# Set-up of a fused residual-stack kernel: W1's loads on ScalarE's queue, E1 products by block, part of the table chain on GpSimd, all weight quarters completed on VectorE

## What is computed

```python
x = x + L0(x, lengths)          # long convolution: K = 2 Re sum_n Cs exp(dtA * l), by head; masked by length
x = x @ W1.T + 2 * gated low-rank term (8 experts, rank 16, top 2 of the logits)
x = x @ W2.T + 0.5 * low-rank term (5 labels, rank 32)
x = x @ (quantised(W3 + delta) + delta).T      # delta = 0.5 * B3 @ A3 (rank 64), thresholds from a 64-entry codebook
```

## Time and profile before

| quantity | value |
|---|---|
| median of 3 runs | 1047.79 us (1047.1 to 1048.24) |
| profiled execution, its own time | 1049.61 us |
| its span | 1047.8 us |
| TensorE busy | 1004.1 us (96%), 4855 instructions |
| VectorE busy | 850.6 us (81%) |
| ScalarE busy | 428.5 us (41%) |
| GpSimd busy | 292.0 us (28%) |
| W1's loads | 8 of 512 KB, median 7.4 us from issue to landing |
| W2's loads | 8 of 512 KB |
| B3 and A3 loads | 2 of 256 KB each |

### The profile page before, as it was taken

One profiled execution on the slowest core, in us unless ns is written; L12 is line 12 of the kernel. 1 busy time (PEld: TensorE's weight loads), 2 busy tenths in 40 slices (PEclk: granted clock), 3 DMA queues, 4 the chain that ended last, 5 costly groups with the idle time before them and its releaser, 6 DMA issues.

```text
span 1047.8 us, 16630 instructions
## 1 busy us (share of the span) xinstructions
PE 1004.1 (96%) x4855; PEld 800.8 (76%) x4855; DVE 850.6 (81%) x1678; ACT 428.5 (41%) x847; POOL 292.0 (28%) x319
## 2 busy tenths in 40 slices
PE   2999999999899999999999999999999999999997
PEld 1555556978688878888888888888888888888885
DVE  5888888979896488878888888888888888888862
ACT  3212222222257454454445444544354535553531
POOL 2200304373435323222332233222322232223100
PEclk9999999999999999999999999999999999999999
DMA  8601000010201335454544455445544454445311
GB/s 257 164 21 61 20 6 35 1 41 1 40 1 21 64 59 104 80 89 75 104 84 84 77 103 87 79 81 97 94 76 84 88 100 74 88 81 103 59 39 41
DMA packets 316659, 74.97 MB, mean 72 GB/s; under 512 B 292490, under 2 KB 309194, under 8 KB 316626
## 3 DMA queue, kind: packets, MB, share of 16 engines
q1 hardware_dynamic: 316626, 74.56, 36.2%
HBM read 57.61 MB, written 16.91 MB: 71 GB/s over the span
## 4 chain that ended last, share of the span: by engine, by line
PE 75%; DVE 10%; issue 9%; ACT 2%; DMA 2%; DVEq 1%; SPq 0%; ACTq 0%
PE bank L647 33%; PE bank L637 10%; PE bank L774 6%; PE bank L823 5%; PE bank L668 4%; PE bank L617 4%; PE bank L606 4%; PE bank L628 3%; DVE quant L1464 3%; PE bank L674 2%; DVE step_t L1459 1%; DVE quant L1505 1%; DVE vq L1478 1%; PE bank L658 1%; DVE quant L1504 1%
## 5 line engine op out<-in xcount | busy, mean ns | idle before, releaser
L647 PE MATMUL bank<-Mh,strips_r 128*128 128x512 f32 x1024 | 289.9, 395 | 0.0
L647 PEld LDWEIGHTS bank<-Mh,strips_r 128*128 128x128 f32 x1024 | 190.7, 188 | 41.5
L475 POOL TENSOR_TENSOR Cl<-QC,Ch 128x256 fp32r<-128x256 f32 x32 | 36.9, 1152 | 454.5 <-ACT Ch L879 454.5
L647 PE MATMUL bank<-Ml,strips_r 128*128 128x512 f32 x512 | 160.6, 395 | 0.0
L897 ACT ACTIVATE SK<-ZZ 64x448 f32<-64x448 f32 x128 | 73.9, 577 | 211.1 <-DVE ZZ L1182 208.7
L1182 DVE SCALAR_TENSOR_TENSOR ZZ<-ZZ,coef 128x192 f32<-128x192 f32 (+1 forms) x256 | 120.3, 510 | 10.1 <-DVE ZZ L1173 0.3
L774 PE MATMUL bank<-E,A 128*128 128x512 f32 (+1 forms) x384 | 126.2, 489 | 0.0
L647 PEld LDWEIGHTS bank<-Ml,strips_r 128*128 128x128 f32 x512 | 96.2, 188 | 22.5
L774 PEld LDWEIGHTS bank<-E,A 128*128 128x128 f32 x384 | 63.9, 192 | 61.8 <-issue 61.8
L637 PE MATMUL bank<-Mh,strips_r 128*128 128x296 f32 x512 | 110.5, 299 | 0.2 <-DVE strips_r L1201 0.2
L1464 DVE TENSOR_TENSOR quant<-quant,step_t 128x1024 f32<-128x1024 f32 x72 | 92.4, 1323 | 0.0
(11 more groups left out here) (279 smaller groups left out, 1733.8 us busy)
## 6 DMA issues: line engine op xcount, KB each, us to landing
X<-in_x SPq DMA_DIRECT2D x256, 64.0 KB, 2.6
XT<-in_x SPq DMA_DIRECT2D x256, 64.0 KB, 2.5
out_x<-O SPq DMA_DIRECT2D x64, 256.0 KB, 3.2
toep<-kpad SPq DMA_DIRECT2D x128, 64.0 KB, 2.1
E<-in_L_cond_W SPq DMA_DIRECT2D x8, 512.0 KB, 7.4
W2s<-in_L_cond_W SPq DMA_DIRECT2D x8, 512.0 KB, 4.4
vq<-in_L_cond_weight SPq DMA_DIRECT2D x8, 512.0 KB, 3.3
LA<-in_L_cond_lora_A SPq DMA_DIRECT2D x8, 80.0 KB, 3.4
```

The lines of the kernel that those rows point to most:

```text
L647: pe.matmul(psO[nh][:, :], xs[:, c, :], ms[:, c, nh * BANK:(nh + 1) * BANK], start=(c == 0 and n == 0), stop=False)
```

## The change

What it does, piece by piece. The eight loads of W1 are issued by ScalarE as its first instructions, each with a semaphore of its own. On SyncE the codebook comes first, then the tables' inputs, B3 once (in rows of 2 KB per partition), the scale as 8 rows of 4 KB, A3 twice, W2's first block, C, the ids, W2's second block, B_lang, W3. The scale is brought to its layout by eight transposes on TensorE (a new job `scale`) and a copy on ScalarE; B3 is transposed in 64 rows and copied twice with a stride. QT(0)'s first 1024 columns become `qt0` in two halves, each block of E1 waited for by itself: the first half stands before the codes and quarter 0's deltas, the second behind them; the B_lang columns stay in `qt` 0. Deltas of quarters 1 to 3 are split in twos; the last two come after `lap`. The transposes `a3` of the next quarter come one M group later. On GpSimd the first exponential of the table chain and its angle are done in 33 small steps (a fused operation of VectorE becomes two) between the diagonals of E1 and A2, `finish_quarter` goes, and A3lo's padding is a memset. VectorE takes the ids' part earlier, waits for GpSimd's angle before the second exponential, completes all four quarters itself, and in `rise_from` waits for the add two instructions back in every case, in place of a wait at the end of each pair. ScalarE does `nat_sine` and quarter 0's initial value after quarter 0's deltas. The kernel rows' products are put in four parts among the products of M group (3, 6).

```diff
-        order = [("b3t", 0), ("b3t", 1), ("codesT",)] + deltas(0) + [("w2t", 0, 0), ("w2t", 0, 1)]
-        between = {0: [("codes",)], 1: [("nat4",), ("at", 0), ("at", 1), ("wrt",)], 2: deltas(1), 5: deltas(2), NC - 1: deltas(3)}
+        order = [("scale",), ("b3t", 0), ("b3t", 1), ("w2t", 0, 0), ("w2t", 0, 1), ("qt0", 0), ("codesT",)] + deltas(0)
+        order += [("qt0", 1), ("codes",)]
+        between = {1: [("nat4",), ("at", 0), ("at", 1), ("wrt",)] + deltas(1)[:2], 2: deltas(1)[2:], 5: deltas(2)[:2], 6: deltas(2)[2:]}
         for kt in range(NC):
             if kt + 1 < NC:
                 order += [("w2t", kt + 1, 0), ("w2t", kt + 1, 1)]
             order += [("qt", kt)] + between.get(kt, [])
-        order += [("a3", 0, n) for n in range(4)] + [("lap", mt) for mt in range(MT)]
+        order += deltas(3)[:2] + [("a3", 0, n) for n in range(4)] + [("lap", mt) for mt in range(MT)] + deltas(3)[2:]
         for q in range(QUARTERS):
             for mt in range(MT + 1):
                 order += [("m", q, mt)]
-                if q + 1 < QUARTERS and mt in (2, 4, 6, 8):
-                    order += [("a3", q + 1, mt // 2 - 1)]
...
+        KERN_IN = 6
...
                 sp.dma_start(cb[:, :], bass.AP(codebook.tensor, 0, [[0, P], [1, K_CODES]])).then_inc(ld_codes, 16)
-                sp.dma_start(scale3[:, :, :], scale_log.rearrange("(t p) g a -> p t (g a)", p=P)).then_inc(ld_codes, 16)
                 sp.dma_start(logs[:, 0:1], log_dt.rearrange("(h a) -> h a", a=1)).then_inc(ld_kgen, 16)
                 sp.dma_start(logs[:, 1:1 + N], log_A_real).then_inc(ld_kgen, 16)
                 sp.dma_start(nat[:, 0, :], A_imag).then_inc(ld_kgen, 16)
-                sp.dma_start(c_in[:, :, :], C_ri).then_inc(ld_kgen, 16)
-                for ot in range(NC):
-                    sp.dma_start(E1[:, ot, 0:L], W1[ot * P:(ot + 1) * P, :]).then_inc(ld_w1, 16)
-
+                sp.dma_start(B3n[:, :, :], B3_lora.rearrange("(p t) r -> p t r", t=NC)).then_inc(ld_b3, 16)
+                sp.dma_start(scale8[:, :], scale_log.rearrange("(t p) g a -> t (p g a)", p=P)).then_inc(ld_scale, 16)
+                for n in range(2):
+                    sp.dma_start(A3raw[n * R3:(n + 1) * R3, :], A3_lora).then_inc(ld_a3, 16)
                 load_w2(0)
+                sp.dma_start(c_in[:, :, :], C_ri).then_inc(ld_c, 16)
...
                 load_w2(1)
...
+                pool.memset(A3lo[R3:, :].bitcast(F32), 0.0).then_inc(a3_pad, 1)
+                pool.wait_ge(a3_pad, 1)
...
-                def finish_quarter(q):
-
-                    for t in range(QT_TILES):
-                        pool.wait_ge(v_used, QT_TILES * q + t + 1)
-                        rounded = qq[q][:, t, :].rearrange("p (g k) -> p g k", g=NC)
-                        step(pool.tensor_tensor(rounded, rounded, scale3[:, q * QT_TILES + t, :].unsqueeze(2).broadcast_to([P, NC, P]), ALU.mult))
-                    pool.tensor_tensor(qq[q][:, :, :], qq[q][:, :, :], dq[q % 2][:, :, :], ALU.add).then_inc(quant_done, 1)
-
-
-
...
-                pool.wait_ge(ld_w1, 16 * NC)
-                for it in range(NC):
+                def madd(out, a, scale, b):
+                    w = out.shape[1]
+                    step(pool.tensor_scalar(nx[:, 6, 0:w], a, scale, None, ALU.mult))
+                    step(pool.tensor_tensor(out, nx[:, 6, 0:w], b, ALU.add))
+
+                def e1_diagonal(it):
+                    pool.wait_ge(ld_w1[it], 16)
                     d = E1[:, it, it * P:(it + 1) * P]
                     pool.tensor_tensor(d, d, ident[:, :], ALU.add).then_inc(e1_ready, 1)
-                for it in range(NC):
+
+                def a2_diagonal(it):
                     pool.wait_ge(stage_free, jobno[("w2t", it, it // 4)] + 1)
                     d = A2[:, it, it * P:(it + 1) * P]
                     pool.tensor_tensor(d, d, ident[:, :], ALU.add).then_inc(a2_ready, 1)
-                    if it == 0:
...
-                    if it == NC - 3:
-                        finish_quarter(0)
-                finish_quarter(1)
+
+
+                t = [nx[:, n, :] for n in range(6)]
+
+                def poly(n):
+                    step(pool.tensor_scalar(t[5], t[5], 1.0 / math.factorial(n), None, ALU.add))
+                    step(pool.tensor_tensor(t[5], t[5], t[4], ALU.mult))
+
+                pool.wait_ge(ld_kgen, 48)
+                step(pool.tensor_scalar(t[0], logs[:, :], -87.0, 88.0, ALU.max, ALU.min))
...
+                madd(t[4], t[2], -LN2_LO, t[3])
+                e1_diagonal(0)
+                pool.wait_ge(e1_ready, 1)
+                step(pool.tensor_scalar(t[5], t[4], 1.0 / math.factorial(7), None, ALU.mult))
+                for n in (6, 5, 4):
+                    poly(n)
+                e1_diagonal(1)
+                a2_diagonal(0)
+                e1_diagonal(2)
+                pool.wait_ge(e1_ready, 3)
+                pool.wait_ge(a2_ready, 1)
+                for n in (3, 2, 1):
+                    poly(n)
+                e1_diagonal(3)
+                pool.wait_ge(e1_ready, 4)
+                step(pool.tensor_scalar(t[5], t[5], 1.0, None, ALU.add))
+                step(pool.tensor_scalar(nx_bits[:, :], t[2], 127.0, float(1 << 23), ALU.add, ALU.mult))
+                step(pool.tensor_tensor(exps[:, :], t[5], nx_bits[:, :].bitcast(F32), ALU.mult))
...
+                e1_diagonal(4)
+                e1_diagonal(5)
+                pool.wait_ge(e1_ready, 6)
+                step(pool.tensor_scalar(turn_n, dtA_im, 1.0 / (2 * math.pi), MAGIC, ALU.mult, ALU.add))
...
+                pool.tensor_tensor(rem_n, rem_n, turn_n, ALU.add).then_inc(nat_rem, 1)
+                pool.wait_ge(nat_rem, 1)
+                e1_diagonal(6)
+                e1_diagonal(7)
+                a2_diagonal(1)
+                pool.wait_ge(ld_blang, 16 * NC)
+                pool.tensor_scalar(E1[:, :, L:EW], E1[:, :, L:EW], 2.0, None, ALU.mult).then_inc(e1_ready, 1)
+                pool.wait_ge(ld_rank, 48)
+                for n in range(3):
+                    pool.tensor_scalar(Bw3[:, :, n * RL:(n + 1) * RL], BwIn[:, :, :], 0.5, None, ALU.mult).then_inc(bw_ready, 1)
+                for it in range(2, NC):
+                    a2_diagonal(it)
...
-                        if j == ("m", 0, 4):
-                            finish_quarter(2)
...
+                def scale_t():
+                    pe.wait_ge(ld_scale, 16)
+                    several(("scale",), NC, lambda ps, g: pe.transpose(ps[:, g * NC:(g + 1) * NC], scale8[:, g::NC], ident[0:NC, 0:NC]))
+
                 def b3t(g):
                     if g == 0:
-                        pe.wait_ge(ld_b3, 64)
+                        pe.wait_ge(ld_b3, 16)
                     several(("b3t", g), 4, lambda ps, n: pe.transpose(
...
+                def qt0(part):
+
+                    if part == 0:
+                        pe.wait_ge(a2_ready, 1)
+                        pe.wait_ge(stage_free, jobno[("w2t", 0, 1)] + 1)
+                    for it in range(part * NC // 2, (part + 1) * NC // 2):
+                        pe.wait_ge(e1_ready, it + 1)
+                        for n in range(2):
+                            pe.matmul(bank[2 + n][:, :], A2[:, it, 0:P], E1[:, it, n * BANK:(n + 1) * BANK], start=(it == 0), stop=(it == NC - 1))
+
...
-                    if kt == 0:
-                        pe.wait_ge(e1_ready, NC)
                     pe.wait_ge(a2_ready, kt + 1)
                     pe.wait_ge(stage_free, jobno[("w2t", kt, 1)] + 1)
                     if kt >= 2:
                         pe.wait_ge(qt_free, kt - 1)
                     s = 2 + 3 * (kt % 2)
                     for n, (a, b) in enumerate(((0, BANK), (BANK, L), (L, EW))):
-                        if kt == 0 and a == L:
+                        if kt == 0 and a < L:
+                            continue
+                        if kt == 0:
 
                             pe.wait_ge(e1_ready, NC + 1)
...
-                def kern():
-
-                    pe.wait_ge(cols_ready, 2)
-                    pe.wait_ge(tab_out, 1)
-                    pe.wait_ge(m_taken, M_LAST)
-                    for h in range(H):
+                def kern(part):
+
+                    if part == 0:
+                        pe.wait_ge(cols_ready, 2)
+                        pe.wait_ge(tab_out, 1)
+                        pe.wait_ge(m_taken, M_LAST)
+                    for h in range(part * H // 4, (part + 1) * H // 4):
                         last = pe.matmul(bank[2][0:SPAN, PARTS * h:PARTS * (h + 1)], Vt[:, h, :], X1T[:, h, 0:PARTS], start=True, stop=True)
-                    last.then_inc(kern_full, 1)
+                    if part == 3:
+                        last.then_inc(kern_full, 1)
...
+                        if (q, mt) == (LAST_Q, KERN_IN) and kt < 4:
+                            kern(kt)
                         last = pe.matmul(m_bank(n)[0:rows, 0:QO], lhs, A3[q % 2][:, kt, :], start=(kt == 0), stop=(kt == NC - 1))
...
```

(40 more changed lines are left out.)

101 lines of the change are left out of this document (53 added, 48 removed).

## The result

The changed kernel takes 1043.3 us (median of 10 runs, 1041.78 to 1045.55) against 1047.44 us for the kernel before (10 runs, 1045.65 to 1050.39) on the same chip. The ratio is 0.9962, 95% interval 0.9948 to 0.9975: 4.1 us faster. The forecast was 15.7 us faster, and the time lies above its range. The profiled execution took 1042.08 us, with a span of 1040.3 against 1047.8 before.

A forecast was written before the change was run, and what follows sets the result against it. Only TensorE's set-up before 400 us was taken to count: its start, two holes and a clock loss. Terms 3.9 + 3.15 + 7.8 + 0.9 = 15.75 us off the median 1047.8 gave 1032.1 us, range 1025 to 1041.

The forecast's parts named there:

- Part 1: Loads and TensorE's start: W2(0) lands near 10.5 us, QT(0) starts at 15, QT(1) near 42; gain 3.9 us.
- 6.1 MB take 15.5 us: Early loads: at 393 GB/s all of them together need 15.5 us, whatever queue issues them.
- My first rival, the late start: Start: W1's backlog holds W2(0), QT(0) starts at 21 us, QT(1) 2 us later than before; 1038 us, chance 0.15.
- the 0.9 us of the kernel rows: M(3,6): kernel-row products put between its column products save 1.8 us or nothing; half taken, 0.9 us.
- The new wait: Before QT(0)'s short records: TensorE waits until about 40.5 us for GpSimd's B_lang scaling, behind W2(1).
- Part 2: Set-up: 33 table-chain steps move to GpSimd at 0.36 us each; gain for TensorE zero.
- the slower rival: Start: GpSimd table steps of 1.95 us delay E1's diagonals, QT(1) 36.3 us late; 1072 us, chance 0.10.
- The cover of 5 us: Start: E1's last diagonal is ready at 24 us, TensorE wants it at 29, so table steps cost TensorE nothing.
- Part 3: Quarters: VectorE completes all, removing the A3b wait (3.15 us) and quarter 3's hole with its slow clock (5.63 + 2.2 us).
- Part 4: Order: deltas split in twos taken at zero; kernel-row products placed among M(3,6)'s column products, 0.9 us.
- If the clock holds: M(3,6): condition under which the M group falls from 5.36 to 3.54 us, saving 1.8 us; otherwise nothing.

The follow-up runs named there:

- The kernel that undoes both (1034.55 us): Changed kernel with B_lang scaled earlier, W1 on SyncE behind W2(0), kernel-row products in one piece, table chain on VectorE, B3 loaded in 128-row blocks: 1034.55 us.
- the one with the start repaired: Changed kernel with B_lang scaled before A2's diagonal 1, W1 on SyncE's queue behind W2(0), kernel-row products in one piece: 1032.38 us, ratio 0.9858.

## Why the prediction was wrong

The direction held, and so did most of the steps behind 46 us. The sum can be laid beside the trace in four stretches:

```
stretch                          forecast gain   measured gain
start to QT(1)                        3.9            -5.6
QT(1) to the A3b products             3.15            5.8
A3b products to M(3,0)                7.8             8.75
M(3,0) to the first output product    0.9            -1.7
sum                                  15.75            7.3
```

So the sum was 8.4 us too high in the profile. The median stands 2.8 us further off, because the two profiled executions lie further apart than the medians.

Of the 5.8 us, 1.7 are a slow clock that the kernel before had behind its QT(1) (1.92 and 16.55 us for what takes 1.07 and 15.68 in the changed one) and that I had not counted; 0.9 more stay open. The 8.75 us include a wait of 0.54 us in front of M(3,0), which is gone too.

**The step that failed is Part 1's: W2(0) lands near 10.5 us, so QT(0)'s first half starts at 15 us.** The first product started at 23.23 us, 8.2 us later. Two things were wrong in this step.

The first is that the two queues would share the engines evenly by bytes, so that 1.4 MB of SyncE's early loads would pass beside W1. By 13 us SyncE's queue had moved 0.58 MB and W1's 2.67. The DMA share of 1.03 in 10 to 20 us says, as in the earlier trace rows, that the engines were full, and 5.54 MB by 20 us fits my "6.1 MB take 15.5 us"; but the turns went by packets here and not by bytes (725 to 597, then 384 to 378). So all of SyncE's loads came late. W2(0) was there at 19.6, when ScalarE's queue had moved nearly all of W1 (4.08 MB of 4.19 by 20 us), and yet the load on the path was a smaller one, the scales at 12.86. The kernel with W1 behind W2(0) in SyncE's queue has the scales by 6.51 and W2(0) by 10.9, about my 10.5, and starts at 18.20: this is 5.0 of the 8.2 us.

The second is the price of what lies between the loads and QT(0), for which I left 4.5 us. The four copies of B3 have a stride and take 4.37 us instead of 2.41, and in the kernels with W1 on SyncE A2's diagonal waits behind GpSimd's table steps. The kernel that undoes both (1034.55 us) starts at 14.82, 3.4 us before the one with the start repaired, and so where I had put the change; ScalarE's copies of A2 end 1.5 us earlier in it (14.43 against 15.97), and the rest is GpSimd's.

My first rival, the late start, with QT(0) at 21 us, was the nearest account of the start. I gave it 0.15 because W2(0) is asked for before half of W1; across the two queues that order did not hold. Its 1038 had QT(1) only 2 us later than before, where it was 5.6, and counted the 0.9 us of the kernel rows.

The Trainium skill, page "DMA: Bandwidth & Descriptors", section "Issuing engines are not separate DMA queues", says that a second issuing engine saves sequencer time and brings no bandwidth. The trace agrees (325 GB/s in 10 to 20 us against 393 before), and the runs go further: the second queue cost 5.0 us. The rule leaves open who goes first when both queues are asked at once, and my sum needed just that. The same page of the Trainium skill, section "Queues, rings and completion order", says that an engine goes round between its queues a packet at a time; the packet counts of the two queues agree with it.

**The new wait was foreseen, its tail was not.** I put GpSimd's B_lang scaling 2.9 us behind TensorE; it was 3.61. From the end of that wait to QT(1) I counted 1.5 us. It was 4.31: the 16 short products ran mostly at the 1.2 GHz level (granted clock 0.57 in 47 to 51, 3.60 us against 1.95 without the wait), and W2(2)'s transposes, 0.9 us, lie between. I had charged such a tail to the quarter-3 hole of the earlier trace rows, and not to the hole that I was adding. With the late start (+8.2), a faster run of TensorE up to that wait (-2.3), the longer wait (+0.7) and this tail (+2.8), QT(1) is 9.4 us behind the forecast 42.

**Part 2, zero:** right for the changed kernel, by the run with the chain back on VectorE. GpSimd's steps took 0.24 to 0.63 us, most 0.3 to 0.4, near the 0.36 taken, so the slower rival's 1.95 us was far off. It is not zero once the loads are in time: there the steps hold A2's diagonal until 17.70. The cover of 5 us that I named had shrunk, though: E1's last diagonal ended at 34.73, the second half of QT(0) began at 34.89. And VectorE's quarter 0 at 39.5 was wrong: it started at 48.86, because the loads (the codebook landed at 6.56, not 3.5) and ScalarE's copies came late. It cost nothing, since quarter 2 waits for deltas(2) anyway.

**Part 3, 3.15 and 7.8 us:** the sum was right and the cause too narrow, which is partly luck: the terms came true because the change contains two cures, of which I priced one. Alone in the kernel before, VectorE's completion gives 9.5 us. Yet the shorter rises and later transposes, without it, give as much, and in the changed kernel, which has these, it gives 2.5. The holes measured how late VectorE was against TensorE's wish (the one at A3b by way of GpSimd, whose dq add for quarter 2 ends at 230.3 before and at 225.6 with the shorter rises), and either cure covers that; their gains don't add. My text put the rises' 2.2 us a quarter and the M group's 3.46 us into the sum of slack and not among the causes, so it could not tell.

**Part 4:** the split of the deltas was nothing, as taken. The kernel rows' 0.9 us did not come. From M(3,0) to the first output product the changed kernel needs 1.7 us more in the profile, and the run in one piece shows the time to be neutral. "If the clock holds" was the condition that failed: it was 0.89 during the split products and 0.50 behind them. What was saved is partly the 0.75 us wait for the Toeplitz blocks at 358.23 of before, which the changed kernel's 350.91 doesn't have.

What stays open: the changed kernel's ten runs lie in two groups, near 1042 and near 1045 us, and in the profiled executions of this study the first half of QT(0) takes between 8.6 and 10.2 us: 8.77 in the changed kernel's of 1042.08 us, 10.02 and 10.18 in the two near 1045 (kernel rows in one piece, tables on VectorE). That would be some 1.3 of the 3 us; it was not tested.

## What to carry to other kernels

Put the loads that the first instructions need into one queue, in the order of need, with the bulk behind them; in this kernel a second queue for the bulk let it overtake them, whatever was asked for first. Then follow the start backwards from its first product: the load that looked late here (W2's first block) was not the one that set it. When a hole is closed, ask by how much the late engine is late in all, since two cures for the same lateness don't add, and price every new wait on TensorE with the slow clock behind it. And when the start gets shorter, look at which load is issued last for the next block.

## What the runs showed of the hardware that I had not expected

Loads of the same form and order took about three times as long to land beside 4.2 MB on another engine's queue: the scales (32 KB) 9.0 us instead of 2.8, B3 8.7 instead of 3.1, A3 11.1 instead of 4.3. ScalarE's copies of 64 x 512 into a layout with a stride of 8 elements took 1.09 us each (four in 4.37), against 0.60 us for the same ones without a stride (four in 2.41, in the kernel of 1034.55 us). And 128 products of 4 columns, in which TensorE counts as busy throughout, left the granted clock at 0.50 afterwards, in one piece or in four.
